# Query distances from four 32-row tiles instead of restacked queries, in an attention and mixture-of-experts kernel

## What is computed

```python
Q, K, V = per-head projections of x                      # 16 heads x 16 channels
L   = K[:, :, landmark_idx]                              # 64 landmarks
Phi_Q = exp(-max(|q|^2 + |l|^2 - 2 q.l, 0) / temperature)   # queries x landmarks
Phi_K = exp(-sq_dists(K, L) / temperature)
W   = exp(-sq_dists(L, L) / temperature) + 1e-6 I
Y   = solve(W, Phi_K^T V);  y1 = solve(W, sum Phi_K)
out = (Phi_Q Y) / max(Phi_Q y1, 1e-10)
x   = layernorm(x + out @ Wo.T + bo)
ids, g = top-2 of (x @ Wg.T + bg), softmax over the two
x   = layernorm(x + sum over the two of g * (x @ We[id].T + be[id]))
```

## Time and profile before

| what | value |
|---|---|
| median of 3 runs | 2026.71 us (2024.04 to 2030.53) |
| profiled execution | 2020.45 us, span 2018.7 us |
| stage one | to about 600 us |
| loop | about 600 to 1530 us |
| expert tiles | about 1530 to 1870 us |
| sum, second norm, store | to the end |
| granted clock of PE, mean | 0.843 of full speed |

### The profile page before, as it was taken

The page is one execution under the profiler, slowest core; times in us unless marked ns, Lnnn a source line. Parts: engine busy times, 40 slices in busy tenths (PEclk is TensorE's granted clock), DMA queues, the critical chain, the costliest instruction groups (busy, mean ns, idle before and its releaser), DMA issues.

```text
span 2018.7 us, 47279 instructions
## 1 busy us (share of the span) xinstructions
PE 1466.8 (73%) x17376; PEld 1176.1 (58%) x17376; DVE 1253.9 (62%) x3459; ACT 1027.5 (51%) x1827; POOL 839.9 (42%) x937
## 2 busy tenths in 40 slices
PE   4578999989986777878777777777537888887000
PEld 3267878777773555555555555555437888886000
DVE  5678844888443566666675767676656555554665
ACT  3256766766656556555655555654222333333444
POOL 2300000000001355555555555555547777777544
PEclk8688999999996888887887888888758999999555
DMA  2585797776856677778777888787446666665999
GB/s 84 95 175 136 173 198 151 175 164 164 179 154 143 147 188 189 189 179 192 181 177 180 190 186 191 186 191 174 122 144 207 210 215 210 210 211 165 340 362 301
DMA packets 321537, 374.96 MB, mean 186 GB/s; under 512 B 73088, under 2 KB 227968, under 8 KB 320896
## 3 DMA queue, kind: packets, MB, share of 16 engines
q1 hardware_dynamic: 295776, 301.63, 61.9%
q0 software_dynamic: 25536, 70.31, 10.0%
HBM read 150.02 MB, written 96.50 MB: 122 GB/s over the span
## 4 chain that ended last, share of the span: by engine, by line
DMA 22%; PE 17%; POOL 15%; SPq 14%; DVE 14%; issue 12%; ACT 4%; ACTq 0%; DVEq 0%; POOLq 0%
POOL terms_dram L710 9%; SPq L468 7%; DMA den_dram<-den_inv 4%; POOL rows_dram L691 4%; DMA q_stack<-kl 3%; PE bank L344 3%; DMA rows_dram<-x,place_i 3%; PE bank L1655 2%; PE bank L345 2%; DMA wel<-kl 2%; PE bank L346 2%; SPq L492 2%; PE bank L1671 2%; DMA out<-phi 2%; PE bank L1656 2%
## 5 line engine op out<-in xcount | busy, mean ns | idle before, releaser
L668 POOL TENSOR_TENSOR xl<-x_raw,xh 128x512 fp32r<-128x512 f32 x60 | 74.9, 1268 | 773.5 <-ACT xh L929 773.5
L691 POOL DMA_INDIRECT rows_dram<-x,place_i x256 | 268.2, 1048 | 91.1 <-issue 69.4
L778 ACT ACTIVATE phi<-bank,invt 128x512 f32<-128x512 f32 x256 | 162.8, 685 | 104.2 <-PE bank L1656 104.0
L914 ACT ACTIVATE phi<-bank,nlt,invt 128x512 f32<-128x512 f32 x256 | 183.1, 773 | 34.1 <-PE bank L1769 33.0
L344 PE MATMUL bank<-weh,q_stack 128*128 x528 | 161.5, 306 | 34.8 <-DVE q_stack L1465 34.4
L1465 DVE TENSOR_TENSOR q_stack<-bank,q_stack 128x512 fp32r<-128x512 f32 x132 | 90.7, 687 | 139.4 <-ACT q_stack L978 138.5
L1655 PE MATMUL bank<-l_hh,k_hl 128*128 128x256 f32 x512 | 145.1, 315 | 39.9 <-DMA k_hl<-kl 26.0
L1122 DVE TENSOR_SCALAR phi<-phi,phi_max,phi_min 128x1024 f32<-128x1024 f32 x128 | 103.7, 810 | 104.2 <-ACT phi L778 103.9
L1273 DVE TENSOR_SCALAR phi<-phi,phi_max,phi_min 128x1024 f32<-128x1024 f32 x128 | 105.8, 831 | 82.0 <-ACT phi L914 82.0
L346 PE MATMUL bank<-wel,q_stack 128*128 x528 | 149.2, 283 | 0.0
L345 PE MATMUL bank<-weh,q_stack 128*128 x528 | 148.7, 282 | 0.0
(11 more groups left out here) (242 smaller groups left out, 4353.5 us busy)
## 6 DMA issues: line engine op xcount, KB each, us to landing
tile_in<-rows_dram SPq DMA_DIRECT2D x264, 130.0 KB
x_raw<-in_xT SPq DMA_DIRECT2D x64, 512.0 KB, 4.8
x_tok<-in_x SPq DMA_DIRECT2D x32, 512.0 KB, 7.4
q_stack<-kh SPq DMA_DIRECT2D x128, 128.0 KB
wel<-kh SPq DMA_DIRECT2D x128, 128.0 KB
attn<-den_dram SPq DMA_DIRECT2D x64, 256.0 KB
phi<-terms_dram SPq DMA_DIRECT2D x22, 512.0 KB, 5.6
out<-phi SPq DMA_DIRECT2D x22, 512.0 KB, 7.8
```

The lines of the kernel that those rows point to most:

```text
L691: nc.gpsimd.indirect_dma_start(out=rows_dram, out_offset=bass.IndirectOffsetOnAxis(ap=place_i[:, at:at + 1].bitcast(u32), axis=0), in_=x1[ ...
L778: nc.scalar.activation(phi[:, n], bank[6 + s][:], ACT.Exp, scale=invt[:]).then_inc(exp_done, 1)
L914: nc.scalar.activation(phi[:, i], bank[6 + i % 2][:], ACT.Exp, bias=nlt[:, c // CPB, i:i + 1], scale=invt[:]).then_inc(qexp_done, 1)
```

## The change

- Queries are no longer stacked. `q_h`, `q_l` and `q_sq` have two buffers of their own, and the distances read them where ACT and DVE wrote them, 32 channels (two heads) at a time. A pair takes four accumulating matmuls over 32 rows: high x high, landmark high x query low, landmark low x query high, and minus ones x squares, the last in plain float32. Four pairs lie in four different row quarters of the array and go to banks 4 to 7.
- The stacking transfers, the query norms on PE and DVE, and the building of stacked landmarks on ACT go away. Masked landmarks are made by two DVE instructions a batch.
- Attention has one bank. ACT copies each half to `attn_raw` (`save_attention`), and the normalisation reads it from there. Denominators move to bank 2, queries to banks 0 and 1.
- Every engine's order in the loop is rewritten. On POOL, the scatters of tiles 2 and 3 of chunk `p - 1` move behind `attn_lo` in the next iteration. On DVE, the normalisation moves behind the places. On SP, the loads of `x` and the inverses change places.
- Expert weights are loaded and split in iterations 2 to 8, and biases in iteration 11.
- The ring of term buffers grows from four to eight.

```diff
-            def query_dists(c, pairs):
...
-                    pe.wait_ge(qexp_done, PAIRS * c + i + 7)
-                    mm(bank[6 + i % 2][:], l_stack[c // CPB % 2][:, i].rearrange("p u k -> p (u k)"), q_stack[c % 2][:, i],
-                       start=True, stop=True).then_inc(qdist_done, 1)
+            def query_dists(c, s):
...
+                pe.wait_ge(ql_done, 2 * c + s + 1)
+                pe.wait_ge(lm_ready, c // CPB + 1)
+                pe.wait_ge(qexp_done, PAIRS * (c + 1) + 4 * s)
+                hi, lo, at = lm_h[c // CPB % 2], lm_l[c // CPB % 2], c % 2
+                wide = lambda a, rows: a[rows, s].rearrange("p u k -> p (u k)")
+                for a, b in ((hi, q_h[at]), (hi, q_l[at]), (lo, q_h[at])):
+                    for j in range(4):
+                        rows = slice(32 * j, 32 * j + 32)
+                        mm(bank[4 + j][:], wide(a, rows), b[rows, s], start=(a is hi and b is q_h[at]), stop=False)
+                for j in range(4):
+                    rows = slice(32 * j, 32 * j + 32)
+                    mm(bank[4 + j][:], neg_pair[rows].rearrange("p u k -> p (u k)"), q_sq[at][rows, s],
+                       start=False, stop=True).then_inc(qdist_done, 1)
```

POOL's, DVE's and PE's orders in an iteration:

```diff
 # POOL
             for p in range(-6, NCH + 1):
                 n, q, a, c = p + 5, p + 3, p + 2, p + 1
+                attn_lo(a - 1, 0)
+                attn_lo(a - 1, 1)
+                scatter(p - 1, 2)
+                scatter(p - 1, 3)
                 if n - 1 > 0:
                     split_lo(n, 1)
                 ln1(c)
-                attn_lo(a, 0)
-                attn_lo(a, 1)
                 scatter(p, 0)
                 scatter(p, 1)
-                scatter(p, 2)
-                scatter(p, 3)
 # DVE
                 q_clamp(q, range(0, 2))
-                q_clamp(q, range(2, 4))
                 residual(c, c % 2)
                 row_stats(c, c % 2)
                 gates_begin(p)
                 choices(p)
+                gates_end(p)
+                find_places(p)
+                q_clamp(q, range(2, 4))
+                q_clamp(q, range(4, 6))
+                q_clamp(q, range(6, 8))
+                normalise_rows(c, c % 2)
                 normalise(a, 0)
-                gates_end(p)
                 normalise(a, 1)
-                find_places(p)
-                q_clamp(q, range(4, 6))
                 queries_lo(n, 0)
                 queries_lo(n, 1)
-                normalise_rows(c, c % 2)
-                q_clamp(q, range(6, 8))
-                query_norms(n)
...
+                invert_denominators(a + 1)
 # PE
+                query_dists(q, 1)
+                logit_transpose(p)
                 attention(q - 1, 1)
+                queries(n, 0)
                 ranks(p)
-                queries(n, 0)
                 queries(n, 1)
...
                 denominators(q, 0)
+                denominators(q, 1)
+                query_dists(q + 1, 0)
...
+                x1_transposes(p + 1, 0)
                 x1_transposes(p + 1, 1)
+                attention(q, 0)
+                output_projection(c + 1, 0)
+                output_projection(c + 1, 1)
                 gate_logits(p + 1)
```

More of the change, by code:

```diff
@@ L188, in program @@
         den_inv = sb("den_inv", [P, P])
-        q_stack = [sb("q_stack0", [P, PAIRS, CH], f32r),
-                   wel[:].rearrange("p k n -> p (k n)").rearrange("p (i n) -> p i n", i=PAIRS)]
-        l_stack = [sb(f"l_stack{i}", [P, PAIRS, 2, NL], f32r) for i in range(2)]
+        lm_h, lm_l = [[sb(f"lm_{n}{i}", [P, KC, 2, NL], f32r) for i in range(2)] for n in "hl"]
+        neg_pair = sb("neg_pair", [P, 2, NL])
+        q_h, q_l, q_sq = ([kh[0], sb("q_h1", [P, KC, CH], f32r)], [kl[0], sb("q_l1", [P, KC, CH], f32r)],
+                          [sq, sb("q_sq1", [P, KC, CH])])
+        attn_raw = sb("attn_raw", [P, KC, CH])
         attn = sb("attn", [P, KC, CH])
@@ L209, in program @@
                                          sb("tile_to", [P, TILES], i32))
-        xt_h, xt_l = [[q_stack[0][:, 2 * a + i] for i in range(2)] for a in range(2)]
-        term = [a[:, k].rearrange("p (u d) -> p u d", u=2) for a in (attn, x1_T) for k in range(KC)]
+        xt_h, xt_l = [[a[:, i] for i in range(2)] for a in (q_h[0], q_l[0])]
+        term = [a[:, k].rearrange("p (u d) -> p u d", u=2) for a in (attn, x1_T, sq, attn_raw) for k in range(KC)]
         def four_rows(a):
@@ L880, in z_landmark_major @@
                 act.wait_ge(y_done, b)
-                nc.scalar.activation(zk[:], bank[4][0:64, :], ACT.Copy).then_inc(zk_ready, 1)
+                nc.scalar.activation(zk[:], bank[3][0:64, :], ACT.Copy).then_inc(zk_ready, 1)
             def queries(c, s):
@@ L965, in weights_hi @@
             def weights_hi(p):
-                if p not in (NCH - 3, NCH - 2):
+                if p not in (FIRST_WEIGHTS + 1, FIRST_WEIGHTS + 5):
                     return
-                k = p - (NCH - 3)
+                k = (p - FIRST_WEIGHTS) // 4
                 for half in range(2):
@@ L1005, in _ @@
                 n, q, a, c = p + 5, p + 3, p + 2, p + 1
-                q_exps(q, range(0, 2))
+                save_attention(q - 1, 0)
                 q_exps(q, range(2, 4))
-                if n - 1 > 0:
-                    query_hi(n, 1)
+                save_logits(p)
+                gate_exp(p)
                 q_exps(q, range(4, 6))
                 q_exps(q, range(6, 8))
-                gate_exp(p)
-                normalise_rows(c, c % 2)
-                attn_hi(a, 0)
-                attn_hi(a, 1)
-                queries(n, 0)
-                queries(n, 1)
-                if begins_batch(q + 1) and q > 0:
-                    z_landmark_major((q + 1) // CPB)
-                if q + 1 == -1:
-                    for g in range(3):
-                        landmarks_of_batch(0, g)
-                    z_landmark_major(0)
+                queries(n, 0)
+                save_attention(q - 1, 1)
+                queries(n, 1)
+                attn_hi(a, 0)
+                if begins_batch(q + 1):
+                    z_landmark_major((q + 1) // CPB)
+                attn_hi(a, 1)
+                normalise_rows(c, c % 2)
+                if n > 0:
+                    query_hi(n + 1, 1)
                 x1_copy(p + 1, 0)
                 x1_copy(p + 1, 1)
-                if q + 1 > 0 and (q + 1) % CPB and not absent(q + 1 + CPB):
-                    landmarks_of_batch((q + 1) // CPB + 1, (q + 1) % CPB - 1)
-                save_logits(p + 1)
+                q_exps(q + 1, range(0, 2))
                 weights_hi(p)
@@ L1811, in attention @@
                     pe.wait_ge(y_ready, (c + 1) // CPB + 1)
-                if c:
-                    pe.wait_ge(attn_ready, 2 * c - 1 + half)
+                pe.wait_ge(attn_saved, 2 * c + half)
                 for j in range(4):
-                    last = mm(bank[4 - half][32 * j:32 * j + 32, :], y_cur[c // CPB % 2][:, 4 * half + j, 0:32],
+                    last = mm(bank[3][32 * j:32 * j + 32, :], y_cur[c // CPB % 2][:, 4 * half + j, 0:32],
                               phi[:, 4 * half + j], start=True, stop=True)
@@ L1972, in shape_constants @@
     c[:, C_PART] = part
+    c[:, C_PAIR:C_PAIR + 2] = part[:, None] // HD % 2 == np.arange(2)
     c[:, C_SPARE:C_SPARE + TAKEN[-1]] = E * REGION + P * (np.arange(TAKEN[-1]) - E)
```

182 lines of the change are left out of this document (70 added, 112 removed).

## The result

The changed kernel takes 1951.6 us, the median of 4 runs (1950.6 to 1952.4), against 2025.4 us for the kernel before on the same chip (2019.3 to 2030.5). The ratio is 0.9637, with a 95% interval of 0.9609 to 0.9665. So it is 74 us faster, where 21.5 us had been forecast, and the time lies 3 us under the range. The profiled execution took 1951.19 us.

What follows compares the result with a forecast made beforehand. The prediction took a loop of waits, the scatter cycle, as the bound, with a new period of 9.2 + 13.5 + 3.9 = 26.6 us. Filling -26.5, loop +11 and tail -6 gave -21.5 us, so 2005 us, range 1955 to 2055 us.

Steps and rivals of the forecast that it cites:

- the scatter cycle: Loop from residual sum through places, scatters and landing to the next residual sum: 26.6 us, the whole interval.
- Places: Residual sum to end of places: 9.2 us against 11.0, a gain of 1.8, with normalisations and attn_lo moved out.
- Scatters: POOL, places to end of the eight scatters: 13.5 us against 10.9, as both attn_lo stand between the halves.
- Landing: Last scatter to next residual sum, waiting for rows: 3.9 us, between 3.1 and 4.7, against 4.7 in mid-loop.
- the spread: SP's transfers spreading the inverses, expected to fall on the landing's moment while 2 MB of stacking a chunk goes.
- Filling: Pipeline start up to chunk 1's residual sum: at 670 us against 696.55, 26.5 us won.
- Tail: After the loop: chunk 31's places wait 3.9 us, not 7.8, and transfers before the first term shorten; 6 us gained.
- Eight term buffers: Expert term stage: POOL's back-to-back scatters are the bound and hide waits for a free buffer; gain 0.
- Row quarters: Distances on PE: 32-row matmuls in four row quarters overlap, 1.55 us a half chunk; serial rival about 2065 us, chance 0.06.
- landing and ranks both at their best: Faster rival in the scatter cycle: 8.3 + 13.5 + 3.1 = 24.9 us, about 1954 us; chance 0.18.
- stretched POOL: Slower rival: DVE's normalisation, reading two SBUF tensors, holds up POOL's scatters; period 27.9 us, time 2044 us; chance 0.08.

Runs made afterwards that it cites:

- a third buffer: Changed kernel with a third buffer of rows and a second place_i, so residual sums wait for the scatters of c - 3: 1873.4 us, ratio 0.9235 to 0.9292.
- the run with all eight together: Changed kernel with all eight scatters of a chunk together on POOL and both attn_lo behind them: 2012.4 us, ratio 0.9912 to 0.9955.
- before reordered: Kernel before, stacking kept, with only normalisations moved behind the places and the scatters of tiles 2 and 3 behind both attn_lo: 2036.7 us, ratio 1.0043 to 1.0093.

## Why the prediction was too cautious

- **What bounds it** (the scatter cycle): right for the changed kernel, 13 of 21 waits and 78 us with a third buffer. For the kernel before, only half of it: DVE idled for the rows in 9 of 20 iterations, and in the others it came to the residual sum too late to wait for them, after waits for ACT. The sum 11.0 + 10.9 + 4.7 met the interval, but a sum that closes doesn't say which of two cycles is the longer.
- **Places** 9.2 us: measured 8.8. In 11 of 20 iterations the ranks ran at full clock (1.0 granted) and it is 8.1 to 8.3 us; in six they ran at half (0.5) and it is 9.1 to 9.4; two at full clock took 11.0 and 12.1 us. The move of the normalisation is shown to be worth 2.2 us of them.
- **Scatters** 13.5 us: measured 13.8. The cost was real, and the run with all eight together shows that it can't be saved for nothing.
- **Landing** 3.9 us, "between 3.1 and 4.7": measured 2.5 us where DVE waited for it, and 3.0 as the mean of all iterations. This is the step that failed. I scaled it by the mean DMA share, 0.79 and 0.42, and took the loop's end as the lower bound. The runs show that the mean share is not the cause: at 0.40 and 0.41 the landing is 4.8 and 2.4 us, and at 0.78 and 0.77 (before, and before reordered) the last row packet comes 3.7 and 2.0 us after the scatters. What decides is how much of the large transfers is still to be moved when the last scatter ends, and so what was issued in the 5 to 6 us before it. The new order alone brings that gain, with the 2 MB that I had put it down to still there. The rows to see it were those of SP beside POOL's last scatter, which I did not set beside each other. I had also put the spread down as a new burden at that moment. It is, but it took the place of a larger one. The lower bound of 3.1 us has no row either: the loop's end shows 3.3.
- Over chunks 3 to 27 the pieces differ from the forecast by -0.4, +0.3 and -0.9 us, together -1.1 us an interval, 33 of the 36.5 us by which the loop missed. The landing is 28 of them.
- **Filling** 26.5 us: measured 33.4, of which some may be chance, as the 12 us spread of that point shows. **Tail** 6 us: measured 10.3; the places of chunk 31 waited 2.06 us rather than 3.9. **Eight term buffers** 0: shown.
- **Row quarters**: together, as assumed. The Trainium skill (TensorE: Matmul & The Clock Gate, Part 3, Measured speedup vs the span model) gives 3.07 times for four row tiles. The 3.1 us that the prediction made of it counted the float32 part of a whole chunk; for a half the estimate by the page is 12 x 0.23 / 3.07 + 4 x 0.86 / 3.07 = 2.0 us. The trace has about 1.8.
- **The rivals**: the nearest is "landing and ranks both at their best", 24.9 us and 1954 us, which I gave 0.18. Its landing of 3.1 us was still too long, and its 8.3 us of places come in about half of the iterations only. That its time lies 2 us from the measured one is luck: its loop is 14.5 us shorter than the measured one (747 against 761.5 us), and filling and tail, which it took as forecast, gave 11 us more. The range began at 1955 us, 1 us above this rival's own value, and so did not take it in as its text says. The stretched POOL did occur in small: the first four scatters take 5.8 us with the normalisations behind the places, 5.2 with them in front.

## What to carry to other kernels

The time from the last of a row of scatters to its landing is not a constant and not a matter of mean DMA load: list what every queue issues in the 6 us before it, and move the large loads behind it. A run whose time doesn't move can still measure such a piece, by the packets, where no engine waits for it. When the pieces of one cycle add up to the period, look whether the engine at its start really idles for it; if it does in half of the iterations only, a second cycle is as long, and removing either alone gains little. An instruction inserted into the bounding cycle can be partly free when a transfer is the next thing to wait for.

## What the runs showed of the hardware

- Eight indirect scatters of 128 rows need 1.6 us from the end of the last on POOL to DVE's next start (their last packet ends after 1.1 us) when nothing else is in flight, 2.5 us with 512 KB issued 3.1 us ahead, 4.8 us with another 512 KB behind it.
- Four 32-row matmuls of 512 columns in reduced float32, in four row quarters, start within 0.02 us and are followed by the next group after 0.23 us at full clock (0.34 behind the first), the 0.23 us of one whole matmul.
- The places' last cast takes 0.17 us now that no `attn_lo` runs beside it, and 0.89 us before. The Trainium skill (SBUF — State Buffer, SBUF: two separate sides) says that DVE and GpSimd share a pair of ports, which one holds for a whole instruction while the other is blocked, for DVE instructions in a two-port mode or, against a GpSimd instruction that reads SBUF, with two SBUF inputs. These rows agree in kind; whether this cast is such an instruction no run here shows.
- On one chip the term scatters took 429 us from first to last where others take 333, and the kernel before was 229 us slower there than elsewhere, more than these 96 us. Whether its four term buffers are the reason was not tried; on the other chips four or eight made no difference.
